# Self-attention on TensorE in steps of two units: score pair, eight transposes, two chunks of head outputs

## The chip, the cores and the metric

The kernel runs on one core of a Trainium2 chip. Times are device microseconds (us) of that core for one execution. Engines are named as the profile names them: PE is TensorE's matmul side (PEld its weight loads), ACT is ScalarE, DVE is VectorE, POOL is GpSimd, SP is SyncE. L485 is line 485 of the kernel before.

## What is computed

The kernel is a decoder of six stages over `x` of shape (4, 512, 128): self-attention, cross-attention, a mixture of experts, a gated decay attention, a second cross-attention and a second mixture of experts, each followed by a residual sum and a layer norm. The change lies in the first stage only:

```python
x = (latents - mu) * jax.lax.rsqrt(var + 1e-05) * ln_gamma + ln_beta
q = (x @ Wq).reshape(b, s, HEADS, DIM_HEAD).transpose(0, 2, 1, 3)    # 16 heads of 64
k = (x @ Wk).reshape(b, s, HEADS, DIM_HEAD).transpose(0, 2, 1, 3)
v = (x @ Wv).reshape(b, s, HEADS, DIM_HEAD).transpose(0, 2, 1, 3)
scores = jnp.einsum('bhqd,bhkd->bhqk', q * scale, k * scale)
weights = jax.nn.softmax(scores.astype(jnp.float32), axis=-1)
out = jnp.einsum('bhqk,bhkd->bhqd', weights, v)
return out.transpose(0, 2, 1, 3).reshape(b, s, HEADS * DIM_HEAD) @ Wo
```

All of it is in fp32.

## The kernel before

The program is written per engine; the order in each engine's block is the order of issue, and semaphores tie the engines together. Nothing reorders instructions between blocks.

**Units and groups.** Self-attention is cut into 256 units: four batches of 64. Unit u is one head and one tile of 128 queries against all 512 keys. Units 2n and 2n+1 are the two heads of a pair on the same query tile. Eight units, a group g = u // 8, are one pair of heads on its four query tiles; there are 32 groups. Below, a place in a group is called j = u % 8, and S(u), X(u), T(u), pt(u) stand for the unit's steps.

**The way of a unit.** S(u): PE makes the scores of both heads of a pair in one go (`a_scores`, L477, called for even u), 4 matmul records of 64 contraction rows. DVE takes the row maximum (`a_max`, L1317). X(u): ACT makes the exponential with its row sum (`a_exp`, L940). DVE inverts the row sum (`a_norm`, L1324), POOL multiplies by it (L1813). T(u): PE transposes the unit's four 128 x 128 squares into one bank (`a_turn`, L489). pt(u): ACT copies that bank to SBUF (`a_pt`, L947). O: PE multiplies with the values (`a_out`, L496), once per group and chunk k of 128 keys, four chunks of 4 matmul records of 64 columns each, into bank 5. ACT copies bank 5 out (`a_o`, L956).

**Banks.** Scores use banks 0 to 2 in rotation, by unit; so S(u) must wait for X(u - 2). Transposes use banks 3 and 4, by u % 2; so T(u) must wait for pt(u - 2) (`take` in L491 puts the wait on `a_pt` in front of it). The projections Q and K (`a_qk`, L471, line L475 in the trace), V (`a_v`, L463, L468), the transposes of the layer norm and the output projection of the batch before (`tail`, L432) share banks 6 and 7 in strict turns (`take_next`, L347): each waits for the copy by ACT of the one issued two before it.

**Order on PE before** (loop at L517): at step u the extra work of that step (a piece of `tail`, Q at j = 2, K at j = 4, V at the steps of `V_STEPS`, L280), then S(u) if u is even, then T(u - 4), then, from step 13 on, chunk (u - 13) % 8 of the head outputs if that is under 4. So chunks 0 to 3 of a group stand at j = 5, 6, 7 and 0.

**Order on ACT** (L976): at step u `tail`, V's copy, X(u), then the copy of Q at j = 2 (`a_q`, `a_evac` L932), of K at j = 5 (`a_k`, the same line), of bank 5 at j = 1, then pt(u - 4). The copy of K for group g + 2 also waits until the last score pair of group g is done, because it overwrites that group's keys.

**Order on DVE** (L1340): at step u first `a_norm(u - 1)`, which waits for X(u - 1), then `a_max(u)`, then `tail` and the layer norm's work.

Of the kernel before, what the change touches and what calls it, by code (L numbers as in the profile page):

```python
# [33 lines left out]
NB = 4  # L34
S = 512
NT = S // P
# [10 lines left out]
UNITS = H * NT  # L47
# [31 lines left out]
def decoder(nc, T):  # L79

    with ExitStack() as ctx:
# [5 lines left out]
        def sem(name):  # L87
            if name not in sems:
                sems[name] = ctx.enter_context(nc.semaphore(name))
            return sems[name]  # L90
# [128 lines left out]
        def v3(ap, n):  # L219
            return ap.rearrange("p (n k) -> p n k", n=n)  # L220


        wqA, wkA, wvA, woA = (W0[:, i * 1024:(i + 1) * 1024] for i in range(4))
# [13 lines left out]
        def out_w(ph):  # L237
            return {0: woA, 1: woB, 3: woD, 4: woE}[ph]

        def o_slot(w, p):  # L240

            if w // NB == 3:
                s = (8 * (w % NB) + p) % 12
                return OT[:, s, :] if s < 8 else oxD[s - 8]
            return OT[:, p, :]
# [27 lines left out]
        def tail_steps(w):  # L273
            if w // NB in (1, 4) and w % NB < NB - 1:
                return (0, 2, 4, 6, 8)

            return TAIL[(w + 1) // NB]


        V_STEPS = ((49, 51, 57, 59), (17, 19, 25, 27))  # L280

        def yn(w):

            return w if w < PC else w - NB

        def out_pieces(w):

            return 4 if w < NB - 1 else 1
# [9 lines left out]
        def loaded(eng, what, n=1):  # L298
            eng.wait_ge(dma_in[what], 16 * n)
# [37 lines left out]
        def take(pe, i, reader, value):  # L337

            if i in owner:
                s, n = owner[i]  # L340
                pe.wait_ge(s, n)
            owner[i] = (reader, value)
            return bank[i]
# [3 lines left out]
        def take_next(pe, key, reader, value):  # L347

            i = 6 + turn[0] % 2
            turn[0] += 1  # L350
            where[key] = bank[i]
            return take(pe, i, reader, value)
# [64 lines left out]
        def _(pe):  # L417
            mm = nc.tensor.matmul

            def tail(w, s, last=False):  # L420

                ph = w // NB
                at = tail_steps(w)
                k, pieces = s - at[0], out_pieces(w)
                if 0 <= k < pieces and ph in (0, 1, 3, 4):
                    n = 4 if ph == 4 else 8
                    if k == 0:

                        pe.wait_ge(sem({0: "a_o", 1: "B_o", 3: "d_og", 4: "E_o"}[ph]), n * (w % NB + 1))
                        take_next(pe, ("y", w), yT_ready, yn(w) + 1)  # L430
                    for p in range(k * n // pieces, (k + 1) * n // pieces):
                        m = mm(where["y", w][:, :], out_w(ph)[:, p * P:(p + 1) * P], o_slot(w, p),  # L432
                               start=(p == 0), stop=(p == n - 1))
                    if k == pieces - 1:
                        m.then_inc(y_ready, 1)
                if s == at[1]:
                    pe.wait_ge(yT_ready, yn(w) + 1)
                    out = take_next(pe, ("yt", w), sem("sum_done"), yn(w) + 1)
                    for t in range(NT):
                        m = nc.tensor.transpose(out[:, t * P:(t + 1) * P], yT[:, t * P:(t + 1) * P], ident)  # L440
                    m.then_inc(yt_ready, 1)
                if s == at[4]:
                    turn_x(w)

            def turn_x(w):

                pe.wait_ge(x_ready, w + 1)
                out = take_next(pe, ("xT", w), xT_ready, w + 1)
                b = w % NB
                for t in range(NT):  # L450
                    m = nc.tensor.transpose(out[:, t * P:(t + 1) * P], x_all[:, 4 * b + t, :], ident)
                m.then_inc(xTp_ready, 1)


            def a_norm_T(b):

                pe.wait_ge(sem("a_xn"), b + 1)
                out = take_next(pe, ("a_xn", b), sem("a_xnT"), b + 1)
                for t in range(NT):
                    m = nc.tensor.transpose(out[:, t * P:(t + 1) * P], v3(xn, NT)[:, t, :], ident)  # L460
                m.then_inc(sem("a_xnp"), 1)

            def a_v(b, hf, t):  # L463

                n = 8 * b + 4 * hf + t
                pe.wait_ge(sem("a_xnT"), b + 1)
                out = take_next(pe, ("a_v", n), sem("a_vs"), n + 1)
                mm(out[:, :], xnT[b % 2][:, t * P:(t + 1) * P], wvA[:, hf * S:(hf + 1) * S], start=True, stop=True)\  # L468
                    .then_inc(sem("a_vp"), 1)

            def a_qk(g, w, ready, done):  # L471
                b, p = g // 8, g % 8
                pe.wait_ge(sem("a_xnT"), b + 1)
                out = take_next(pe, (ready, g), sem(done), g + 1)
                mm(out[:, :], w[:, p * P:(p + 1) * P], xnT[b % 2], start=True, stop=True).then_inc(sem(ready), 1)  # L475

            def a_scores(u):  # L477
                g, t = u // 8, (u // 2) % 4
                if u % 8 == 0:

                    pe.wait_ge(sem("a_qe"), g + 1)
                    pe.wait_ge(sem("a_ke"), g + 1)
                out = [take(pe, (u + hh) % 3, sem("a_e"), u + hh + 1) for hh in range(2)]
                for hh in range(2):
                    m = mm(out[hh][:, :], qA[g % 2][HALF[hh], t * P:(t + 1) * P], kA[g % 2][HALF[hh], :],  # L485
                           start=True, stop=True)
                m.then_inc(sem("a_s"), 1)

            def a_turn(u):  # L489
                pe.wait_ge(sem("a_n"), u + 1)  # L490
                out = take(pe, 3 + u % 2, sem("a_pt"), u + 1)  # L491
                for k in range(NT):
                    m = nc.tensor.transpose(out[:, k * P:(k + 1) * P], pA[u % 5][:, k * P:(k + 1) * P], ident)  # L493
                m.then_inc(sem("a_t"), 1)

            def a_out(g, k):  # L496
                b, p = g // 8, g % 8
                if k == 0:
                    pe.wait_ge(sem("a_pt"), 8 * g + 8)
                    pe.wait_ge(sem("a_vs"), 8 * b + 4 * (p // 4) + 4)  # L500
                    take(pe, 5, sem("a_o"), g + 1)
                for hh in range(2):
                    m = mm(bank[5][hh * DH:(hh + 1) * DH, :], v3(vA[p // 4], NT)[:, k, (2 * (p % 4) + hh) * DH:(2 * (p % 4) + hh + 1) * DH],  # L503
                           v3(ptA[(2 * g + hh) % 4], NT)[:, k, :], start=(k == 0), stop=(k == NT - 1))
                if k == NT - 1:
                    m.then_inc(sem("a_pv"), 1)
# [7 lines left out]
            for t in range(NT):  # L514
                a_v(0, 0, t)
            NU = NB * UNITS
            for u in range(NU + 9):  # L517
                b, s, g, j = u // UNITS, u % UNITS, u // 8, u % 8
                if u < NU:
                    if u == UNITS:  # L520
                        loaded(pe, "woA")
                    if b:
                        tail(b - 1, s)
                    if s == 30 and b + 1 < NB:
                        a_norm_T(b + 1)
                    if j == 2 and g + 1 < 32:
                        a_qk(g + 1, wqA, "a_qp", "a_qe")
                    if j == 4 and g + 2 < 32:
                        a_qk(g + 2, wkA, "a_kp", "a_ke")
                    if s in V_STEPS[0] and b + 1 < NB:  # L530
                        a_v(b + 1, 0, V_STEPS[0].index(s))
                    if s in V_STEPS[1]:
                        a_v(b, 1, V_STEPS[1].index(s))
                    if u % 2 == 0:
                        a_scores(u)
                if 4 <= u < NU + 4:
                    a_turn(u - 4)
                if u >= 13:

                    h, k = divmod(u - 13, 8)  # L540
                    if k < NT and h < 32:
                        a_out(h, k)


# [1439 lines left out]
```

## Time and profile before

| what | us |
|---|---|
| median of 3 runs (1633.65 to 1636.2) | 1636.05 |
| the profiled execution, its own time | 1640.13 |
| its span, from the first to the last instruction | 1638.3 |
| self-attention, from the first score pair to the last head outputs | about 21 to 550 |

Of the span PE is busy for 1328.1 us (81%), DVE for 854.0, ACT for 831.8 and POOL for 546.9. A line of the timeline reads: start, time from that start to the end of the last instruction merged into the line, engine, line, operation, output <- input, forms, count, and in brackets the idle time of the engine before it with what ended it. The ends of matmuls are modelled and overlap the next matmul; the distance between two starts is what the first one holds the engine for.

### The profile page before, as it was taken

The page shows a single profiled execution, that of the slowest core. Times are in us where ns is not written, and L with a number is a line of the kernel's source. Part 1 is how long each engine was busy: PE and PEld are TensorE (multiplying, and loading weights), DVE is VectorE, ACT ScalarE, POOL GpSimd, SP SyncE. Part 2 cuts the span into 40 slices and gives each one's busy share as a digit, 9 for nine tenths or more (in the row PEclk, how much of TensorE's full clock was granted, in tenths as well). Part 3 has the DMA queues.
Part 4 walks back from the last instruction along what each step waited for, and adds up shares of the span by engine and source line. Part 5 has one row for each costly group of instructions (what it writes and reads, how often), then busy time and mean ns, then how long its engine had stood idle before and what let it go on. Part 6 is the DMA issues. An engine that isn't in the chain of part 4 may idle for free.

```text
span 1638.3 us, 22200 instructions
## 1 busy us (share of the span) xinstructions
PE 1328.1 (81%) x6934; PEld 743.1 (45%) x6934; DVE 854.0 (52%) x2721; ACT 831.8 (51%) x1885; POOL 546.9 (33%) x511
## 2 busy tenths in 40 slices
PE   5999999999999888876549658788889897796460
PEld 2434434444443345444248636455555554444250
DVE  3444543453344354674522176777666775557525
ACT  4777677677677535453225345446454552343130
POOL 3455455455445411323454342100000110112253
PEclk9999999999999989987769879889999997887685
DMA  9000000000000000000259600000000000000172
GB/s 371 23 1 1 1 1 1 1 1 1 1 1 1 1 0 1 1 1 13 85 187 339 222 26 9 6 1 1 1 1 1 1 1 0 1 1 7 37 234 59
DMA packets 35074, 67.30 MB, mean 41 GB/s; under 512 B 5424, under 2 KB 21296, under 8 KB 33808
## 3 DMA queue, kind: packets, MB, share of 16 engines
q1 hardware_dynamic: 29328, 54.37, 9.6%
q0 software_dynamic: 5056, 10.36, 2.1%
q8 instruction: 58, 0.95, 0.2%
q10 hardware_dynamic: 576, 1.16, 0.2%
q14 instruction: 56, 0.46, 0.1%
HBM read 47.71 MB, written 18.15 MB: 40 GB/s over the span
## 4 chain that ended last, share of the span: by engine, by line
PE 60%; DVE 19%; issue 8%; ACT 5%; DMA 5%; POOL 2%; DVEq 0%; ACTq 0%; POOLq 0%
PE bank L503 8%; PE bank L485 7%; PE bank L493 6%; PE bank L432 5%; DMA work<-xs,xi 4%; PE bank L608 3%; PE bank L806 3%; PE bank L475 3%; PE bank L565 3%; PE bank L579 3%; PE bank L802 2%; DVE work L1321 2%; PE bank L594 1%; PE bank L672 1%; POOL xs L1866 1%
## 5 line engine op out<-in xcount | busy, mean ns | idle before, releaser
L1813 POOL TENSOR_TENSOR work<-work 128x512 f32<-128x512 f32 x256 | 266.5, 1041 | 277.6 <-DVE work L1329 277.6
L944 ACT ACTIVATE work<-bank,work 128x512 f32<-128x512 f32 x256 | 176.5, 689 | 117.8 <-DVE work L1321 117.6
L1321 DVE TENSOR_REDUCE work<-bank 128x1 f32<-128x512 f32 x256 | 176.7, 690 | 76.7 <-PE bank L485 75.8
L493 PEld LDWEIGHTS bank<-cst,work 128*128 128x128 f32 x1024 | 110.5, 140 | 164.4 <-issue 106.0
L493 PE MATMUL bank<-cst,work 128*128 128x128 f32 x1024 | 160.0, 283 | 6.6 <-ACT work L952 6.1
L1329 DVE RECIPROCAL work<-work 128x1 f32<-128x1 f32 x256 | 41.9, 164 | 222.6 <-ACT work L944 222.3
L952 ACT ACTIVATE work<-bank 128x512 f32<-128x512 f32 x256 | 152.6, 596 | 0.5 <-PE bank L493 0.5
L1914 POOL TENSOR_TENSOR work<-work 128x512 f32<-128x512 f32 x32 | 40.9, 1277 | 332.4 <-PE bank L806 312.6
L485 PE MATMUL bank<-work 64*128 64x512 f32 x512 | 144.5, 641 | 3.4 <-ACT work L944 3.4
L1853 POOL TENSOR_TENSOR work<-work 128x1232 f32<-128x1232 f32 (+1 forms) x32 | 55.5, 1735 | 250.3 <-DVE work L1401 250.2
L503 PE MATMUL bank<-work 128*64 128x512 f32 x512 | 137.4, 617 | 0.7 <-ACT work L952 0.7
L1383 DVE TENSOR_REDUCE work<-bank 128x6 f32<-128x462 f32 (+1 forms) x80 | 38.9, 536 | 111.7 <-PE bank L579 111.6
L1108 ACT ACTIVATE work<-bank,W 128x128 f32<-128x128 f32 x202 | 58.6, 368 | 75.3 <-PE bank L672 63.3
L432 PE MATMUL bank<-OT,W 128*128 128x512 f32 x208 | 94.0, 595 | 0.7 <-DVE am L1506 0.7
L594 PE MATMUL bank<-cst,work 128*128 128x128 f32 x384 | 60.8, 311 | 28.2 <-POOL work L1853 20.8
L485 PEld LDWEIGHTS bank<-work 64*128 64x128 f32 x512 | 38.7, 184 | 97.0 <-issue 60.5
L1055 ACT ACTIVATE work<-bank 128x512 f32<-128x512 f32 x96 | 53.1, 595 | 54.7 <-PE bank L594 54.2
L1148 ACT ACTIVATE work<-bank,work 128x128 f32<-128x128 f32 x256 | 72.4, 384 | 14.5 <-PE bank L754 10.1
L763 PE MATMUL bank<-W_low 128*128 128x512 f32 x96 | 46.8, 487 | 40.6 <-DVE work L1643 19.2
L1893 POOL DMA_INDIRECT work<-xs,xi x62 | 58.7, 947 | 61.6 <-PE bank L663 45.3
L475 PE MATMUL bank<-W 128*128 128x512 f32 x128 | 68.1, 617 | 6.2 <-ACT work L932 3.9
L579 PE MATMUL bank<-work 128*128 128x154 f32 x384 | 60.5, 309 | 13.8 <-DVE work L1388 13.8
(232 smaller groups left out, 2550.0 us busy)
## 6 DMA issues: line engine op xcount, KB each, us to landing
W<-in_wC SPq DMA_DIRECT2D x39, 578.0 KB
xs<-gat SPq DMA_DIRECT2D x9, 1024.0 KB, 16.5
W<-in_wF SPq DMA_DIRECT2D x23, 321.0 KB
ys<-work SPq DMA_DIRECT2D x62, 64.0 KB
x_all<-in_x SPq DMA_DIRECT2D x4, 256.0 KB, 8.7
W<-in_L_attn_Wq SPq DMA_DIRECT2D x2, 512.0 KB, 5.5
W<-in_L_attn_Wv SPq DMA_DIRECT2D x2, 512.0 KB, 7.6
W<-in_L_attn_Wo SPq DMA_DIRECT2D x2, 512.0 KB, 9.0
```

The costliest lines, as they stand in the source:

```text
L432: m = mm(where["y", w][:, :], out_w(ph)[:, p * P:(p + 1) * P], o_slot(w, p), start=(p == 0), stop=(p == n - 1))
L475: mm(out[:, :], w[:, p * P:(p + 1) * P], xnT[b % 2], start=True, stop=True).then_inc(sem(ready), 1)
L485: m = mm(out[hh][:, :], qA[g % 2][HALF[hh], t * P:(t + 1) * P], kA[g % 2][HALF[hh], :], start=True, stop=True)
L493: m = nc.tensor.transpose(out[:, k * P:(k + 1) * P], pA[u % 5][:, k * P:(k + 1) * P], ident)
L503: m = mm(bank[5][hh * DH:(hh + 1) * DH, :], v3(vA[p // 4], NT)[:, k, (2 * (p % 4) + hh) * DH:(2 * (p % 4) + hh + 1) * DH], v3(ptA[(2 * g + ...
L579: m = mm(out[:, (p % 3) * 2 * C:(p % 3 + 1) * 2 * C], v3(qTB, NPAIR)[:, p, t * P:(t + 1) * P], kd, start=True, stop=True)
L594: m = nc.tensor.transpose(out[:, i * P:(i + 1) * P], pB[u % 3][:, h * C:h * C + P], ident)
L944: A(pA[u % 5], bank[u % 3][:, :], ACT.Exp, bias=nmax[:, u % 8:u % 8 + 1], accum_out=rsum[0][:, u % 8:u % 8 + 1]).then_inc(sem("a_e"), 1)
L952: A(v3(ptA[h % 4], NT)[:, :, t * P:(t + 1) * P], v3(bank[3 + u % 2][:, :], NT), ACT.Copy)\
L1148: i = A(dmD[g % 2][:, (NT * hh + c) * P:(NT * hh + c + 1) * P], bank[1 - hh][:, c * P:(c + 1) * P], ACT.Exp, scale=-1.0, bias=lcD[b % 2][: ...
L1321: V.tensor_reduce(nmax[:, u % 8:u % 8 + 1], bank[u % 3][:, :], AX, ALU.max, negate=True)\
L1813: G.tensor_tensor(pA[u % 5], pA[u % 5], rsum[1][:, u % 8:u % 8 + 1].to_broadcast([P, S]), ALU.mult)\
```

## The change

Only PE's loop changes. It now runs over even u. A step does the extra work of step u and of step u + 1 (the same calls, in the same order among themselves, V ahead of Q and K within one), then S(u), then T(u - 4) and T(u - 3) with nothing between them, then, at j = 6, chunks 0 and 1 of the head outputs, and at j = 0, chunks 2 and 3. ACT, DVE, POOL and SP keep their instructions and their order, and no bank, buffer or wait is another.

```diff
-            for u in range(NU + 9):
-                b, s, g, j = u // UNITS, u % UNITS, u // 8, u % 8
+            for u in range(0, NU + 10, 2):
+                b, g = u // UNITS, u // 8
                 if u < NU:
                     if u == UNITS:
                         loaded(pe, "woA")
-                    if b:
-                        tail(b - 1, s)
-                    if s == 30 and b + 1 < NB:
-                        a_norm_T(b + 1)
-                    if j == 2 and g + 1 < 32:
-                        a_qk(g + 1, wqA, "a_qp", "a_qe")
-                    if j == 4 and g + 2 < 32:
-                        a_qk(g + 2, wkA, "a_kp", "a_ke")
-                    if s in V_STEPS[0] and b + 1 < NB:
-                        a_v(b + 1, 0, V_STEPS[0].index(s))
-                    if s in V_STEPS[1]:
-                        a_v(b, 1, V_STEPS[1].index(s))
-                    if u % 2 == 0:
-                        a_scores(u)
-                if 4 <= u < NU + 4:
-                    a_turn(u - 4)
-                if u >= 13:
-
-                    h, k = divmod(u - 13, 8)
-                    if k < NT and h < 32:
+                    for s in (u % UNITS, u % UNITS + 1):
+                        if b:
+                            tail(b - 1, s)
+                        if s == 30 and b + 1 < NB:
+                            a_norm_T(b + 1)
+                        if s in V_STEPS[0] and b + 1 < NB:
+                            a_v(b + 1, 0, V_STEPS[0].index(s))
+                        if s in V_STEPS[1]:
+                            a_v(b, 1, V_STEPS[1].index(s))
+                        if s % 8 == 2 and g + 1 < 32:
+                            a_qk(g + 1, wqA, "a_qp", "a_qe")
+                        if s % 8 == 4 and g + 2 < 32:
+                            a_qk(g + 2, wkA, "a_kp", "a_ke")
+                    a_scores(u)
+                for v in (u - 4, u - 3):
+                    if 0 <= v < NU:
+                        a_turn(v)
+                h, i = divmod(u - 14, 8)
+                if 0 <= h < 32 and i in (0, 2):
+
+                    for k in (i, i + 1):
                         a_out(h, k)
```

What stands on PE in a row, in a group without V (here units 34 to 39 of the first batch). L485 is a score pair, L493 x4 one unit's transposes, L475 Q or K, L503 x2 one chunk of the head outputs. Before:

```order
L485 MATMUL bank<-work 128x512 x2
L493 MATMUL bank<-cst,work 128x128 x8
L475 MATMUL bank<-W 128x512
L485 MATMUL bank<-work 128x512 x2
L493 MATMUL bank<-cst,work 128x128 x8
L503 MATMUL bank<-work 64x512 x2
L485 MATMUL bank<-work 128x512 x2
L493 MATMUL bank<-cst,work 128x128 x4
L503 MATMUL bank<-work 64x512 x2
L493 MATMUL bank<-cst,work 128x128 x4
L503 MATMUL bank<-work 64x512 x2
```

The same place on PE in the changed kernel:

```order
L485 MATMUL bank<-work 128x512 x2
L493 MATMUL bank<-cst,work 128x128 x8
L475 MATMUL bank<-W 128x512
L485 MATMUL bank<-work 128x512 x2
L493 MATMUL bank<-cst,work 128x128 x8
L485 MATMUL bank<-work 128x512 x2
L493 MATMUL bank<-cst,work 128x128 x8
L503 MATMUL bank<-work 64x512 x4
```

Between the third-last and the second-last score pair (j = 4 and j = 6) a chunk has gone; behind the pair at j = 6 the chunk that stood between the two units' transposes has moved behind both.

The second place is PE's beginning of a group with V (units 16 to 20; L468 is V). Before:

```order
L485 MATMUL bank<-work 128x512 x2
L493 MATMUL bank<-cst,work 128x128 x4
L503 MATMUL bank<-work 64x512 x2
L468 MATMUL bank<-W 128x512
L493 MATMUL bank<-cst,work 128x128 x4
L475 MATMUL bank<-W 128x512
L485 MATMUL bank<-work 128x512 x2
L493 MATMUL bank<-cst,work 128x128 x4
L468 MATMUL bank<-W 128x512
L493 MATMUL bank<-cst,work 128x128 x4
L475 MATMUL bank<-W 128x512
L485 MATMUL bank<-work 128x512 x2
```

And in the changed kernel:

```order
L468 MATMUL bank<-W 128x512
L485 MATMUL bank<-work 128x512 x2
L493 MATMUL bank<-cst,work 128x128 x8
L503 MATMUL bank<-work 64x512 x4
L475 MATMUL bank<-W 128x512
L468 MATMUL bank<-W 128x512
L485 MATMUL bank<-work 128x512 x2
L493 MATMUL bank<-cst,work 128x128 x8
L475 MATMUL bank<-W 128x512
L485 MATMUL bank<-work 128x512 x2
```

Each V has moved from behind a score pair to the front of it: the first to the front of S at j = 0, the second to the front of S at j = 2, straight behind Q.

## Rows read from the trace of the kernel before

**Rows 1.** Busy time by stretch: us, each engine's busy us, granted clock, DMA.
```profile
21.00:550.00 529.00, 513.86 (x2298) 210.95 (x2298) 233.08 (x659) 385.37 (x899) 266.71 (x257) 1.00 0.05 19
600.00:640.00 40.00, 33.91 (x166) 20.78 (x167) 18.01 (x31) 22.65 (x33) 8.99 (x4) 0.91 0.00 1
```

**Rows 2.** Timeline of PE, a group without V: start, us, operation, [idle <- releaser].
```profile
280.70 1.13 PE L485 MATMUL bank<-work 64*128 64x512 f32 x4
...
284.80 1.13 PE L485 MATMUL bank<-work 64*128 64x512 f32 x4
285.86 1.09 PE L493 MATMUL bank<-cst,work 128*128 128x128 f32 x8
286.79 1.02 PE L475 MATMUL bank<-W 128*128 128x512 f32 x2
287.75 1.13 PE L485 MATMUL bank<-work 64*128 64x512 f32 x4
...
289.76 0.63 PE L493 MATMUL bank<-cst,work 128*128 128x128 f32 x4 [0.29 <-ACT work L952]
290.31 1.08 PE L503 MATMUL bank<-work 128*64 128x512 f32 x4
291.32 1.13 PE L485 MATMUL bank<-work 64*128 64x512 f32 x4
...
295.57 0.70 PE L485 MATMUL bank<-work 64*128 64x512 f32 x2
```

**Rows 3.** Timeline of ACT in the same group.
```profile
286.70 0.69 ACT L944 ACTIVATE work<-bank,work 128x512 f32<-128x512 f32 x1 [0.74 <-DVE work L1321]
...
287.38 0.59 ACT L932 ACTIVATE work<-bank 128x512 f32<-128x512 f32 x1
...
288.34 0.70 ACT L944 ACTIVATE work<-bank,work 128x512 f32<-128x512 f32 x1
...
289.00 0.61 ACT L952 ACTIVATE work<-bank 128x512 f32<-128x512 f32 x1
289.96 0.69 ACT L944 ACTIVATE work<-bank,work 128x512 f32<-128x512 f32 x1 [0.35 <-DVE work L1321]
...
292.56 0.60 ACT L932 ACTIVATE work<-bank 128x512 f32<-128x512 f32 x1 [0.20 <-PE bank L485]
```

**Rows 4.** Timeline of PE and ACT in a group with V.
```profile
112.42 1.13 PE L485 MATMUL bank<-work 64*128 64x512 f32 x4
...
118.98 1.02 PE L468 MATMUL bank<-W 128*128 128x512 f32 x2
119.84 0.60 PE L493 MATMUL bank<-cst,work 128*128 128x128 f32 x4
...
120.01 0.59 ACT L932 ACTIVATE work<-bank 128x512 f32<-128x512 f32 x1
...
120.74 1.10 PE L475 MATMUL bank<-W 128*128 128x512 f32 x2 [0.30 <-ACT work L932]
...
122.83 1.09 PE L493 MATMUL bank<-cst,work 128*128 128x128 f32 x8
123.85 1.08 PE L503 MATMUL bank<-work 128*64 128x512 f32 x4
...
129.11 0.70 PE L485 MATMUL bank<-work 64*128 64x512 f32 x2
```

**Rows 5.** Timeline at the start, where no head outputs lie between transposes and scores.
```profile
26.67 0.69 ACT L944 ACTIVATE work<-bank,work 128x512 f32<-128x512 f32 x1 [0.82 <-DVE work L1321]
...
27.59 1.13 PE L485 MATMUL bank<-work 64*128 64x512 f32 x4 [1.10 <-ACT work L944]
...
30.79 1.13 PE L485 MATMUL bank<-work 64*128 64x512 f32 x4 [1.04 <-ACT work L944]
```

**Rows 6.** Timeline of PE in cross-attention: head outputs in one run.
```profile
681.76 3.96 PE L608 MATMUL bank<-work 128*64 128x512 f32 x16
685.65 2.36 PE L579 MATMUL bank<-work 128*128 128x154 f32 x16
```

## The prediction

> **What bounds the kernel now.** I read the busy times by stretch first, then the timeline of one group of eight units on PE and on ACT, then the places where PE is known to wait. In self-attention PE is busy for 513.86 of 529 us at a granted clock of 1.00, full speed [rows 1]. So PE's own order sets the time there, and what it waits for is small: in a group without V one wait, for the copy pt of ACT in front of the second unit's transposes, [0.29 <-ACT work L952] [rows 2]. A group without V lasts 295.57 - 280.70 = 14.87 us from score pair to score pair [rows 2], one with V 129.11 - 112.42 = 16.69 us [rows 4]. The rest of the program is not touched.
>
> Behind PE stands a second cycle that is nearly as long. X of one unit, the inverse and the next maximum on DVE, then X of the next: 286.70 to 288.34 to 289.96, that is 1.64 and 1.62 us per unit [rows 3], or 13.0 us per group against PE's 14.87. A change that lets PE wait on this cycle at one point and leaves it nothing to do meanwhile loses quickly.
>
> **Prices, from starts to starts.** Score pair to transposes 1.06 (284.80 to 285.86), two units' transposes 0.93 (285.86 to 286.79), Q or K ahead of scores 0.96 [rows 2]. Two units' transposes ahead of head outputs 1.02 (122.83 to 123.85), a projection ahead of an operation of the full array 0.86 (118.98 to 119.84) [rows 4]. One chunk of head outputs 1.01 (290.31 to 291.32), transposes that had to wait 0.55 (289.76 to 290.31) [rows 2]. Two chunks in one run are not in this stage; cross-attention runs four of the same shape in 685.65 - 681.76 = 3.89, which makes 1.95 for two [rows 6]; the ends are 1.89 (a little less switching) and 2.02 (nothing saved). I take 1.95.
>
> The waits: X(u) starts 1.90 after the start of S(u) (284.80 to 286.70) [rows 2, 3]. A score pair can follow X(u - 2) by 0.92 (26.67 to 27.59) [rows 5]. X holds ACT for 0.68 (286.70 to 287.38), a copy for 0.48 (287.38 to 288.34 holds two) [rows 3]. Transposes can follow the start of the copy that frees their bank by 0.76 (289.00 to 289.76) [rows 2, 3]. K can follow the start of Q's copy by 0.73 (120.01 to 120.74) [rows 4].
>
> **What the change saves.** In a group without V the order is now S TT OO, Q S TT, K S TT, S TT OO. Without any wait that is (1.06 + 1.02 + 1.95 + 0.96) + (1.06 + 0.93 + 0.96) + (1.06 + 0.93) + (1.06 + 1.02 + 1.95) = 4.99 + 2.95 + 1.99 + 4.03 = 13.96, which is 0.91 less than 14.87: about half of it the wait, the rest fewer changes between score, output and full-array matmuls.
>
> **What it costs, group without V.** I follow one group with S at j = 0 at time 0.
> - S(2) at 4.99 (X(0) at 1.90 frees it long before). X(2) at 6.89, X(3) 1.64 later at 8.53, X(4) 1.62 later at 10.15.
> - S(4) at 7.94, its transposes; PE has nothing left at 9.93. Before, a chunk of head outputs lay here. S(6) needs X(4): 10.15 + 0.92 = 11.07, a wait of 1.14. The start of the trace shows this very pattern, two score pairs with only transposes between, 3.20 apart (27.59 to 30.79) with [1.04 <-ACT work L944] [rows 5].
> - X(5) at 11.77; ACT then copies K (12.45) and pt(1) (12.93). K's copy waited 0.20 for the score pair before [rows 3]; now S(6), at 11.07, is early enough, since the copy could follow it by 292.56 - 291.32 = 1.24 [rows 2, 3], at 12.31.
> - T(2) at 12.13, T(3) would come at 12.62, but its bank is free only at 12.93 + 0.76 = 13.69: a wait of 1.07. Before, chunk 1 stood between the two and covered it. The chunks now queue behind T(3), although they are ready.
> - Output chunks at 13.69 + 0.55 = 14.24, next group at 14.24 + 1.95 = 16.19.
>
> So 16.19 against 14.87: **+1.32 per group**. The waits (2.21) are more than the saving (0.91). Nothing later in the group makes it up, because X(6) and X(7) run ahead of the next S. Who waits for the late T(3)? Its pt and the next S(0), and with it everything.
>
> **Group with V.** The first V stands ahead of S(0), the second between Q and S(2). OO ends at 4.03, Q 0.86, V 0.96: S(2) at 5.85 instead of 5.01. V's bank is free by then (its copy on ACT starts about 3.06). X(2) at 7.75, Q's copy at 8.43, K at 8.43 + 0.73 = 9.16, while PE has been ready since 5.85 + 1.06 + 0.93 = 7.84: a wait of 1.32, where the kernel before had 119.84 + 0.44 to 120.74, some 0.46, because V stood behind the pair. S(4) at 10.12, X(4) 12.02, S(6) 12.94, X(5) 13.64, K's copy 14.32, pt(1) 14.80, T(3) 15.56, outputs 16.11 to 18.06, the next V 0.96: 19.02. Against 16.69: **+2.33 per group**.
>
> **The sum.** V is at 14 groups (two per batch for the second half, two more in three batches for the first). Three groups carry pieces of the output projection, which stand ahead of the score pairs and cover the first wait; I give them 0.3 each. Groups 0, 1 and 31 fill and drain the pipeline; the first two run at the X cycle already, the last has the T wait: 1 us in all. The other 12 are plain. 12 x 1.32 + 14 x 2.33 + 1 + 1 = 15.8 + 32.6 + 2 = 50.4 us. The profiled execution would go from 1640.1 to 1690.5. The median of the runs lies 4.1 lower, so 1636.05 + 50.4 = **1686**. The ends of the unknown price of OO are -0.06 and +0.07 on 26 groups, 2 us; that V groups with layer norm work on DVE lose less takes off up to 10.
>
> **Rivals.**
> 1. *The switches are what costs, and PE stays ahead (faster).* Were the waits on ACT absent, each of 26 groups would give 0.91 back: 24 us, 1612. It decides where the two waits per group stay under 0.91. For it: PE is 97% busy [rows 1]. Against it: the wait of 0.29 that is there already with more cover, and the 1.04 at the start [rows 2, 5]. The Trainium skill, TensorEngine Tiling (Array Packing), section Key Properties, says that changing the tiling mode drains TensorE, which speaks for this rival; the rows agree with a small size: transposes for two units take 0.93 ahead of a full-array operation [rows 2] and 1.02 ahead of outputs [rows 4].
> 2. *Only the score wait counts.* If T(3) does not wait (ACT frees its bank in time, because X(5) comes sooner than I have it), each of 26 groups keeps 1.07 of the loss: 28 us less, 1658.
> 3. *PE's clock falls.* With gaps of over 1 us twice a group the granted clock could drop as it does at 600 to 640, 33.91 of 40 busy and 0.91 [rows 1]. At 0.91 some 18% of the stretch runs at half speed (1.2 of 2.4 GHz), up to 529 x 0.18 / 2 = 48 us more: 1734. Against it: gaps of 1.04 to 1.10 at the start stand within the stretch that keeps 1.00 [rows 1, 5]. The Trainium skill, TensorE: Matmul & The Clock Gate, tells of kernels whose clock swings because PE idles briefly between groups while banks cycle; by that the time would be this rival's, and the trace so far does not show it for gaps of this size.
>
> **Chances.** The forecast 0.86, the first rival 0.05, the second 0.05, the third 0.04. A measurement of this kernel can tell 0.2% (3.3 us) from no change. Slower by more: 0.93 (forecast, second and third, less a little for a mix of the first two); within 0.2%: 0.02; faster: 0.05. The range, 1656 to 1702, takes the forecast with its ends and reaches the second rival.
>
> **What the profile after would show.** In a group without V: S at j = 4 and j = 6 about 3.1 apart with an idle PE released by ACT L944 (its line then one lower); T at j = 6 in two runs 1.6 apart, the second released by the copy pt; groups of 16.2 and 19.0; K released by Q's copy after some 1.3; a clock of 1.00; everything behind self-attention as before but 50 us later. I am wrong if the second transposes start 0.5 behind the first at j = 6, if groups are under 14.9, or if the clock in self-attention is below 1.00.

## The result

| kernel | median us | runs | ratio to before, 95% interval |
|---|---|---|---|
| before | 1636.12 | 1633.65 to 1641.84 | |
| changed | 1690.6 | 1690.08 to 1692.51 | 1.033 (1.0302 to 1.0358) |

The change costs 54.5 us of the median; 50.4 were forecast (1686, range 1656 to 1702). All of it is in self-attention. From the first score pair to the last head output the stage took 531.3 us before and takes 585.1 now, 53.9 more. The first score pair starts 1.0 later, and the rest of the program behind the stage, the same code, took 1085.5 us before and 1080.5 after, so the span grew by 50.0 only; in the eleven kernels of this study that rest lies between 1077 and 1086. That the 50.0 of the span come so near to the 50.4 forecast is therefore chance; the stage's 53.9 is the number to set beside it. Below, kernels are compared by the stage and by the group of eight units, and their medians beside it.

Busy times by stretch of the changed kernel, to set beside [rows 1]: PE does as many instructions (x2298) in 583 us as before in 529, its busy time has even fallen a little, and the clock has stayed at 1.00.

```profile
21.00:604.00 583.00, 510.32 (x2298) 217.65 (x2296) 231.58 (x659) 381.58 (x899) 266.08 (x256) 1.00 0.04 17
```

Who PE waited for in the stage, in the changed kernel (engine, tile and line, releaser: us in total, times, longest):

```profile
PE bank L493 <- ACT work L953: 31.6, 47, 0.9
PE bank L485 <- ACT work L945: 20.3, 33, 1.1
PE bank L475 <- ACT work L933: 16.2, 14, 1.2
PE bank L468 <- ACT xT_all L908: 3.8, 3, 1.7
```

Before, the three first lines held 6.1, 3.4 and 3.9 us. Each is one wait that the prediction named: transposes for their bank (pt), score pairs for an exponential, K for Q's copy. The fourth it did not name.

A group without V on PE, timeline of the changed kernel (columns as in [rows 2]; ACT's lines are one higher than before):

```profile
308.55 1.13 PE L485 MATMUL bank<-work 64*128 64x512 f32 x4
...
316.50 1.13 PE L485 MATMUL bank<-work 64*128 64x512 f32 x4
317.56 0.66 PE L493 MATMUL bank<-cst,work 128*128 128x128 f32 x4
318.51 0.63 PE L493 MATMUL bank<-cst,work 128*128 128x128 f32 x4 [0.29 <-ACT work L953]
319.64 1.13 PE L485 MATMUL bank<-work 64*128 64x512 f32 x4 [0.50 <-ACT work L945]
320.70 0.66 PE L493 MATMUL bank<-cst,work 128*128 128x128 f32 x4
322.23 0.63 PE L493 MATMUL bank<-cst,work 128*128 128x128 f32 x4 [0.87 <-ACT work L953]
322.79 1.94 PE L503 MATMUL bank<-work 128*64 128x512 f32 x8
324.65 1.13 PE L485 MATMUL bank<-work 64*128 64x512 f32 x4
```

From pair to pair 324.65 - 308.55 = 16.10 us, against 14.87 [rows 2]. The pairs at j = 4 and j = 6 stand 3.14 apart (316.50, 319.64), with only transposes between; the transposes at j = 6 come in two runs 1.53 apart (320.70, 322.23), and the chunks queue behind the second. Before, the pair at j = 6 came 3.57 behind the one at j = 4, but a chunk was done in between [rows 2]. The bracket shows less than the whole wait, because the modelled end of the matmul before it reaches into it; starts are what to go by.

Why the second transposes are late stands on ACT:

```profile
318.71 0.69 ACT L945 ACTIVATE work<-bank,work 128x512 f32<-128x512 f32 x1 [0.35 <-DVE work L1322]
...
320.33 0.69 ACT L945 ACTIVATE work<-bank,work 128x512 f32<-128x512 f32 x1 [0.35 <-DVE work L1322]
...
321.01 0.59 ACT L933 ACTIVATE work<-bank 128x512 f32<-128x512 f32 x1
321.48 0.60 ACT L953 ACTIVATE work<-bank 128x512 f32<-128x512 f32 x1
```

X(4) at 318.71 releases the pair at 319.64, 0.93 later; X(5), K's copy, then pt(1) at 321.48, and the transposes 0.75 behind it.

The third wait, in a group with V, from the timeline of PE; the last line is ACT's copy of Q there:

```profile
127.52 1.13 PE L485 MATMUL bank<-work 64*128 64x512 f32 x4
128.58 1.09 PE L493 MATMUL bank<-cst,work 128*128 128x128 f32 x8
130.83 1.10 PE L475 MATMUL bank<-W 128*128 128x512 f32 x2 [1.16 <-ACT work L933]
131.85 1.13 PE L485 MATMUL bank<-work 64*128 64x512 f32 x4
...
130.10 0.59 ACT L933 ACTIVATE work<-bank 128x512 f32<-128x512 f32 x1
```

K (L475) starts 0.73 behind the start of Q's copy. Eight transposes hold PE for 0.93, so it was ready at 129.51 and stood for 1.32.

### The profile page after: what moved, and what is told of

Read it like the earlier page. It is cut to its first block, busy times and chain, and to the rows that moved or that the text cites. A ratio compares the mean times of both kernels' runs of the same rounds, so it can differ in the third digit from the quotient of the medians.

```text
span 1688.3 us, 22200 instructions
## 1 busy us (share of the span) xinstructions
PE 1320.0 (78%) x6934; PEld 748.9 (44%) x6934; DVE 853.2 (51%) x2721; ACT 827.8 (49%) x1885; POOL 545.9 (32%) x511
## 4 chain that ended last, share of the span: by engine, by line
PE 53%; DVE 21%; issue 10%; ACT 8%; DMA 6%; POOL 2%; DVEq 0%; ACTq 0%; POOLq 0%
PE bank L503 7%; PE bank L432 5%; PE bank L485 5%; DMA work<-xs,xi 5%; DVE work L1322 4%; PE bank L493 3%; PE bank L807 3%; PE bank L475 3%; PE bank L609 3%; PE bank L566 3%; ACT work L945 3%; PE bank L580 3%; PE bank L803 2%; PE bank L468 2%; ACT work L933 2%
## 5 line engine op out<-in xcount | busy, mean ns | idle before, releaser
L493 PE MATMUL bank<-cst,work 128*128 128x128 f32 x1024 | 150.0, 281 | 32.3 <-ACT work L953 31.6
L493 PEld LDWEIGHTS bank<-cst,work 128*128 128x128 f32 x1024 | 108.7, 140 | 140.5 <-issue 103.5
L485 PE MATMUL bank<-work 64*128 64x512 f32 x512 | 144.5, 639 | 20.3 <-ACT work L945 20.3
L503 PE MATMUL bank<-work 128*64 128x512 f32 x512 | 123.8, 605 | 0.7 <-ACT work L953 0.7
L475 PE MATMUL bank<-W 128*128 128x512 f32 x128 | 71.8, 647 | 18.5 <-ACT work L933 16.2
L485 PEld LDWEIGHTS bank<-work 64*128 64x128 f32 x512 | 39.5, 184 | 100.8 <-issue 52.7
L595 PE MATMUL bank<-cst,work 128*128 128x128 f32 x384 | 59.3, 305 | 26.6 <-POOL work L1854 19.1
L1149 ACT ACTIVATE work<-bank,work 128x128 f32<-128x128 f32 x256 | 72.3, 384 | 14.9 <-PE bank L755 10.5
## 6 DMA issues: line engine op xcount, KB each, us to landing
xs<-gat SPq DMA_DIRECT2D x9, 1024.0 KB, 16.2
```

The source lines that it names most:

```text
L595: m = nc.tensor.transpose(out[:, i * P:(i + 1) * P], pB[u % 3][:, h * C:h * C + P], ident)
L1149: i = A(dmD[g % 2][:, (NT * hh + c) * P:(NT * hh + c + 1) * P], bank[1 - hh][:, c * P:(c + 1) * P], ACT.Exp, scale=-1.0, bias=lcD[b % 2][: ...
```

## The experiments

The length of a group is from the start of its first score pair to that of the next group's; "with V" is such a stretch that holds two V's; the stage is from the first score pair to the last head output, against 531.3 before, in one profiled execution of each kernel. Each kernel's runs share a chip with runs of the kernel before.

| kernel | median (before beside it) | stage vs before | plain group | with V |
|---|---|---|---|---|
| before | | 0 | 14.88 | 16.69 |
| changed | 1690.6 (1636.1) | +53.9 | 16.10 | 19.10 |
| e1 alternating | 1674.6 (1634.3) | +39.8 | 15.64 | 18.64 |
| e2 extra work behind | 1670.3 (1634.3) | +36.8 | 16.10 | 18.04 |
| e3 copies paired | 1659.8 (1634.3) | +28.4 | 15.53 | 18.04 |
| e4 chunks at j = 4 | 1682.5 (1634.3) | +51.8 | 16.10 | 18.04 |
| e9 both cures | 1654.7 (1636.3) | +18.3 | 14.84 (two of 15.19) | 17.10 |
| e8 only extra work in front | 1659.2 (1633.9) | +23.3 | 14.88 | 17.70 |
| e5 rebalanced | **1607.7** (1633.9) | **-27.8** | 13.79 | 15.51 |
| e6 rebalanced, chunks at j = 6 | 1636.6 (1633.9) | +2.1 | 15.04 | 16.45 |
| e7 rebalanced, alternating | 1624.6 (1633.9) | -11.5 | 14.39 | 16.11 |

**e1: transposes and chunks alternate.**

```diff
-                for v in (u - 4, u - 3):
-                    if 0 <= v < NU:
-                        a_turn(v)
-                h, i = divmod(u - 14, 8)
-                if 0 <= h < 32 and i in (0, 2):
-                    for k in (i, i + 1):
-                        a_out(h, k)
+                h, i = divmod(u - 14, 8)
+                for v, k in ((u - 4, i), (u - 3, i + 1)):
+                    if 0 <= v < NU:
+                        a_turn(v)
+                    if 0 <= h < 32 and i in (0, 2):
+                        a_out(h, k)
```

> The changed kernel with one thing undone: within a step the transposes and the chunks alternate again, T(u-4), chunk, T(u-3), chunk, at j = 6 and j = 0. Steps of two units, their extra work in front, and the places of the chunks by step stay. My theory (the two waits on ACT): the wait of T at j = 6 for its bank (1.07 per group) is covered by the chunk, S at j = 6 still waits for X at j = 4; a plain group falls from 16.10 to about 15.56, one with V by 0.63, in all 26 x 0.6 = 15 us less than the changed kernel: 1675. Rival A (the longer runs are worth something in themselves and the loss lies in the work moved in front of the pairs): nothing gained, and 0.15 per change of mode lost on 64 places, 1690 to 1700. Rival B (the run of eight transposes is the whole loss): back to 1640.

Measured 1674.6, ratio 1.0234 (1.0212 to 1.0255), 16 us under the changed kernel, 14 by the stage. A chunk now stands between the two units' transposes at j = 6; the step S(6) to S(0) fell from 5.01 to 4.25, and PE's waits for pt in the stage from 31.6 to 6.0 us, what they were before. The wait of the pair at j = 6 stayed: 3.14, 20.2 us in all. So the wait for the bank is real, it is worth 0.76 per group less the 0.30 that alternating costs at j = 0, and it is not the whole loss.

**e2: the odd unit's extra work behind the pair.** The extra work of step u stays in front of S(u), that of u + 1 goes behind the chunks.

```diff
-                    for s in (u % UNITS, u % UNITS + 1):
-                        ...
+                    extra(u, u % UNITS)
                     a_scores(u)
...
                         a_out(h, k)
+                if u < NU:
+                    extra(u, u % UNITS + 1)
```

> The changed kernel with one thing undone: the extra work of the odd unit of a step (V, pieces of the output projection, copies' transposes) stands behind the step's score pair, transposes and chunks, not in front of the pair. Transposes and chunks stay in runs. My theory: plain groups stay at 16.1; a group with V loses one projection's 0.96 of delay, since the first V is now covered by the wait of the copies and K waits less for Q's copy; 14 x 0.96 = 13 us less: 1677. Rival A (the work moved in front of the pairs is the whole loss): about 1640. Rival B (only the runs matter): unchanged, 1690.

Measured 1670.3, ratio 1.0212 (1.0194 to 1.023), 20 us under the changed kernel, 17 by the stage, where 13 were expected. The groups behaved as worked out: plain 16.10, with V 19.10 to 18.04, and PE's wait of K for Q's copy fell from 16.2 to 3.0 us in the 14 groups. What I had left out is that the groups of units 24 to 31 in the second and third batch, where the new x of the batch before is transposed, and those with the output projection gain too, 20.35 to 19.06 and 23.27 to 22.38.

**e3: the two copies paired on ACT.** PE is as in the changed kernel.

```diff
-                if u >= 4:
-                    a_pt(u - 4)
+                if u >= 4 and u % 2 == 0:
+                    a_pt(u - 4)
+                    a_pt(u - 3)
```

> PE as in the changed kernel. On ACT the two copies of a pair of transposed units, pt(u-4) and pt(u-3), now both stand behind X(u), in the time in which ACT waits for the second maximum, instead of one behind X(u) and one behind X(u+1). My theory (T waits for its bank, that is for pt): T at j = 6 no longer waits (1.07 less), though X(3) comes 0.5 later behind Q's copy, so that S at j = 6 waits 0.5 longer; a plain group 16.1 to 15.6, one with V 19.1 to 18.0; 7 + 15 = 22 us less than the changed kernel: 1668. Rival C (the weight loads in front of the transposes, put down to POOL by the trace, wait for POOL's product and not for the bank): nothing changes, 1690.

Measured 1659.8, ratio 1.0149 (1.0126 to 1.0171), 31 us under the changed kernel by the medians, 25.5 by the stage, where 22 were expected. PE's timeline in a plain group:

```profile
304.65 1.13 PE L485 MATMUL bank<-work 64*128 64x512 f32 x4
305.71 1.09 PE L493 MATMUL bank<-cst,work 128*128 128x128 f32 x8
308.28 1.13 PE L485 MATMUL bank<-work 64*128 64x512 f32 x4 [1.48 <-ACT work L945]
309.34 1.09 PE L493 MATMUL bank<-cst,work 128*128 128x128 f32 x8
```

Transposes run eight in a row at j = 4 and j = 6, and no transposes wait for a copy any more in the stage's list. The wait for the pair at j = 6 grew from 3.14 to 3.63 between starts, as Q's copy and two pt's now lie ahead of X(3). The rival is out: POOL's work is as before, and the waits of the transposes are gone. The trace still puts 47.0 us of the weight loads' idle time in front of the transposes down to POOL (37.1 in the changed kernel), though the matmuls behind them now start without a wait; so that line does not show what holds the transposes up.

**e4: chunks 0 and 1 at j = 4.**

```diff
-                h, i = divmod(u - 14, 8)
-                if 0 <= h < 32 and i in (0, 2):
-                    for k in (i, i + 1):
+                h, i = divmod(u - 12, 8)
+                if 0 <= h < 32 and i in (0, 4):
+                    for k in (i // 2, i // 2 + 1):
```

> The changed kernel with chunks 0 and 1 in the step j = 4 instead of j = 6; they stay in one run, as all else. My theory: S at j = 6 no longer waits for X at j = 4, as 1.9 us of work stand in between (1.14 less); T at j = 6 still waits for its bank, longer than before, because the copy of K now waits for the later score pair; a plain group about 15.5, one with V 18.0; 7 + 13 = 20 us less: 1670. Rival B (the run of eight transposes is the whole loss): nothing changes, 1690. If both of my waits can be had at once, this and the paired copies add up.

Measured 1682.5, ratio 1.0281 (1.0262 to 1.03): 8 us gained where 20 were expected; in the stage 2. Two short falls of the clock are in it (last section). The wait for the score pair went as expected (20.3 to 6.8 us in the stage), but a plain group stayed at 16.10. Timeline of PE:

```profile
252.85 1.13 PE L485 MATMUL bank<-work 64*128 64x512 f32 x4
253.91 0.66 PE L493 MATMUL bank<-cst,work 128*128 128x128 f32 x4
254.95 0.63 PE L493 MATMUL bank<-cst,work 128*128 128x128 f32 x4 [0.39 <-ACT work L952]
...
265.81 1.13 PE L485 MATMUL bank<-work 64*128 64x512 f32 x4
266.87 0.66 PE L493 MATMUL bank<-cst,work 128*128 128x128 f32 x4
268.28 0.63 PE L493 MATMUL bank<-cst,work 128*128 128x128 f32 x4 [0.75 <-ACT work L952]
```

and of ACT at the same place:

```profile
267.05 0.60 ACT L932 ACTIVATE work<-bank 128x512 f32<-128x512 f32 x1 [1.06 <-PE bank L485]
267.54 0.59 ACT L952 ACTIVATE work<-bank 128x512 f32<-128x512 f32 x1
```

The pair at j = 6 is now at 265.81, later behind the one at j = 4 than before, and K's copy on ACT waits 1.06 for it (it must not overwrite keys in use). pt(1) and everything else on ACT stand behind that copy. This I had counted at j = 6; that ACT carries the delay on into the next group, where the second transposes at j = 0 wait as well (253.91 to 254.95), I had not, and it is the missing 0.6 of the group. Of the cures tried on the changed kernel this one shows best that a wait removed on PE can come back through an in-order engine beside it.

**e9: e3 and e4 together.**

> The changed kernel with both cures at once, and nothing else: chunks 0 and 1 in the step j = 4, and the two copies of transposes both behind X(u) on ACT. Q, K, V and the extra work of odd units stay where the change has them. My theory: the chunks at j = 4 alone brought little because T then waited longer for its bank (behind K's copy, which waits for the later score pair); with the copies paired that wait is gone and the two cures add up to more than their sum. From the measured prices: plain group, X(2) at 6.81, X(4) at 10.55, S(6) at 11.81 without a wait, X(6) at 13.81, next group at 14.73; group with V 16.9. That is 12 x -0.1 + 14 x 0.25 against the kernel before, and 6 us for the work moved in front at the layer norm's and output projection's places: about 1642. Rival (the cures overlap: one wait is what counts, and it is gone with the paired copies): as the paired copies alone, 1660.

Measured 1654.7, ratio 1.012 (1.0093 to 1.0146). The groups are as worked out, 14.84 (14.73 expected) and 17.10 or 16.98 (16.9): a plain group gains 1.26, more than twice the 0.57 that e3 alone and the nothing that e4 alone bring it. So in the plain groups the cures do more together than apart, and the rival, in which one wait is all, is wrong there. The 1642 was missed by 13 us, most of it where the layer norm's and the output projection's work stands in front of a pair: the two groups of units 24 to 31 in the second and third batch take 22.0 and 22.8 us against 17.9 before, those with the output projection 23.4 against 22.0. I had given these places 6 us. Two short falls of the clock, told of at the end, are in it.

**e8: only the extra work in front.** The kernel before, with transposes and chunks unit by unit as they were, but the extra work of u and u + 1 in front of S(u). The edit is shown against the changed kernel.

```diff
-                for v in (u - 4, u - 3):
-                    if 0 <= v < NU:
-                        a_turn(v)
-                h, i = divmod(u - 14, 8)
-                if 0 <= h < 32 and i in (0, 2):
-
-                    for k in (i, i + 1):
-                        a_out(h, k)
+                for v in (u, u + 1):
+                    if 4 <= v < NU + 4:
+                        a_turn(v - 4)
+                    if v >= 13:
+                        h, k = divmod(v - 13, 8)
+                        if k < NT and h < 32:
+                            a_out(h, k)
```

> The kernel before with one part of the change alone: the extra work of unit u + 1 stands with that of u in front of the score pair; transposes and chunks stay where they were, unit by unit. My theory: plain groups stay at 14.9; a group with V loses about one projection less what the K wait had cost before, 0.9: 14 x 0.9 = 13 us, and 4 us at the places of the layer norm's and output projection's transposes: 1651. Rival (it costs only beside the longer runs): 1634.

Measured 1659.2, ratio 1.0158 (1.0128 to 1.0188): +25 us where +17 were expected, +23 in the stage. Plain groups did not change (14.88), those with V went from 16.69 to 17.70, and the groups ahead of one, which now hold its first V, from 14.87 to 15.94, with K's wait for Q's copy at 15.2 us in the stage, against 3.9. The rest is at the odd places. Timeline of PE and ACT at unit 26 of the second batch:

```profile
210.04 0.60 PE L451 MATMUL bank<-cst,x_all 128*128 128x128 f32 x4
210.70 1.10 PE L475 MATMUL bank<-W 128*128 128x512 f32 x2
214.04 1.10 PE L468 MATMUL bank<-W 128*128 128x512 f32 x2 [2.24 <-ACT xT_all L907]
215.06 1.65 PE L485 MATMUL bank<-work 64*128 64x512 f32 x4
```

```profile
211.65 0.69 ACT L944 ACTIVATE work<-bank,work 128x512 f32<-128x512 f32 x1 [1.10 <-DVE work L1321]
...
213.29 0.61 ACT L907 ACTIVATE xT_all<-bank 128x512 f32<-128x512 f32 x1
```

V of unit 27 (L468) needs the bank that the transposes of the new x at unit 26 (L451, `turn_x`) hold until ACT copies them (L907). ACT does that at its own step 26, behind the exponential of unit 25, while PE already stands in front of the score pair of unit 26. With V behind the pair, as before, the wait fell into time that PE had work for. It is K's wait for Q's copy once more, with another pair of users of banks 6 and 7.

**e5: rebalanced.** If the two waits and the bank turns are the loss, the runs of the change should pay once all are covered. On PE chunks 0 and 1 at j = 4, Q in front of j = 0, K in front of j = 4, odd units' work behind the pair; on ACT the copies paired and the others behind the second exponential of a pair:

```diff
-        V_STEPS = ((49, 51, 57, 59), (17, 19, 25, 27))
+        V_STEPS = ((51, 55, 59, 63), (19, 23, 27, 31))
...
-                        if s % 8 == 2 and g + 1 < 32:
+                if s % 8 == 0 and g + 1 < 32:
...
+                    a_exp(u)
+                    if j == 1 and g >= 2:
+                        a_o(g - 2)
+                    if j == 1 and g + 1 < 32:
+                        a_q(g + 1)
+                    if j == 5 and g + 2 < 32:
+                        a_k(g + 2)
...
+                if u >= 4 and u % 2 == 0:
+                    a_pt(u - 4)
+                    a_pt(u - 3)
```

> Runs of eight transposes and of two chunks, as in the change, but with both waits covered: the two copies of transposes both behind X(u) on ACT; chunks 0 and 1 at j = 4, chunks 2 and 3 at j = 0; Q in front of the pair at j = 0 and K in front of that at j = 4, so that each step without chunks is followed by a projection; the extra work of odd units behind the pair; V at odd units 3 and 7 of its groups; ACT copies Q and bank 5 behind X at j = 1, K behind X at j = 5. My theory: with the waits covered PE is the bound again and the fewer changes between kinds of matmul show: a plain group 13.9 (4.0 + 2.95 + 4.0 + 2.95) against 14.87 before, one with V 15.6 to 15.8 against 16.69: 12 x 0.95 + 14 x 1.0 = 25 us less than before, 1609. Rival (the cycle of exponential and maximum, 1.63 per unit and 13.0 per group, leaves no slack and binds at other places): within 8 us of before.

Measured 1607.7, ratio 0.9839 (0.9815 to 0.9863): 26 us faster than before, 83 faster than the changed kernel, with the change's runs in it. Timeline of PE over a plain group:

```profile
268.56 1.13 PE L485 MATMUL bank<-work 64*128 64x512 f32 x4
269.62 1.09 PE L493 MATMUL bank<-cst,work 128*128 128x128 f32 x8
270.64 1.94 PE L503 MATMUL bank<-work 128*64 128x512 f32 x8
272.51 1.13 PE L485 MATMUL bank<-work 64*128 64x512 f32 x4
...
282.35 0.70 PE L485 MATMUL bank<-work 64*128 64x512 f32 x2
```

None of PE's lines in this group, those left out included, has a bracket: every start follows from the instruction before it, and 282.35 - 268.56 = 13.79 us per group.

**e6: the same with chunks 0 and 1 back at j = 6.**

> As the rebalanced kernel, but chunks 0 and 1 back at j = 6, where the change has them. My theory: T no longer waits for its bank, but S at j = 6 again waits for X at j = 4, as only transposes lie between: from S at j = 2 to S at j = 6 6.08 (1.90 + 1.64 + 1.62 + 0.92), a plain group about 14.9 against 13.9, 1.0 more on 26 groups: 26 us more than the rebalanced kernel, about 1635. Rival (only the transposes' bank mattered): as the rebalanced kernel.

Measured 1636.6, ratio 1.0012 (0.9997 to 1.0028), 29 us more than e5; a plain group 15.04 against 14.9 expected. PE's waits for exponentials in front of score pairs are 33.8 us in the stage, against 7.9 in e5, and there is none for transposes. So the cover of the score pair at j = 6, taken alone, is worth 1.25 us a plain group.

**e7: the same as e5, alternating.**

> As the rebalanced kernel, but transposes and chunks alternate again within a step (T, chunk, T, chunk). This measures what the longer runs are worth where nothing waits. My theory: 0.14 for the first chunk's way out and 0.15 for the second transposes' way in, 0.30 per run (5.31 against 5.01 for the step at j = 0 in the runs with and without), two runs per group, 0.6 per group: 32 x 0.6 = 19 us more than the rebalanced kernel, about 1628. Rival (the runs are worth nothing in themselves, the gain of the rebalanced kernel is the wait that the kernel before had): same as the rebalanced kernel.

Measured 1624.6, ratio 0.9943 (0.9926 to 0.9961), 17 us more than e5; 16.2 in the stage. Where nothing waits, two units' transposes and two chunks take 3.19 us alternating and 2.89 in runs (283.94 to 287.13 in e7, 269.62 to 272.51 in e5), 0.30 a time and 0.60 a group. So of the 26 us by which e5 is faster than the kernel before, the longer runs gave some 17; the other 9 (11.5 in the stage) come with e7 too, from the places of the other work:

```profile
283.94 0.66 PE L493 MATMUL bank<-cst,work 128*128 128x128 f32 x4
284.52 1.08 PE L503 MATMUL bank<-work 128*64 128x512 f32 x4
285.53 0.66 PE L493 MATMUL bank<-cst,work 128*128 128x128 f32 x4
286.12 1.08 PE L503 MATMUL bank<-work 128*64 128x512 f32 x4
287.13 1.13 PE L485 MATMUL bank<-work 64*128 64x512 f32 x4
```

## Why the prediction was right, point by point

- **The saving.** 0.91 per plain group was the forecast, half of it fewer changes between kinds of matmul. The e5 group, which has none of the waits, is 1.09 shorter than before, 0.60 of it shown by e7 to be the runs. Two chunks in one run took 1.86 (322.79 to 324.65), not 1.95; the lower end of the range, 1.89, was nearer.
- **The score pair at j = 6** waits for X(4): 3.14 between the pairs, 3.13 forecast (7.94 to 11.07). Shown by e6 against e5.
- **The second transposes at j = 6** wait for their bank: 1.53 between the two runs, 1.56 forecast. Shown by e1 and e3, the second of which left PE alone.
- **K waits for Q's copy** in a group with V: 1.32 (129.51 to 130.83), 1.32 forecast. Shown by e2, which puts V behind the pair again and leaves 3.0 of 16.2 us, and by e8, which brings 15.2 us of it into the kernel before.
- **A plain group** 16.10 against 16.19, **one with V** 19.10 against 19.02. (The working has 5.01 once where its own sum gives 4.99; nothing hangs on it.) The 12 plain groups grew by 14.2 in all, where 15.8 were forecast.
- **The groups with V** hold the first term that was mis-sized. 2.33 each counts both V's, but a group's first V now stands in front of its S(0), and so in the stretch of the group ahead: 17.16 for group 5, 16.10 for a plain one, 1.06 for the V. Booked to V in all seven such places, the eight groups without layer norm or output work of the batch before cost 18.4 together, against 18.6. The six with it (groups 2 and 3 of the second to fourth batch) cost 18.0, against 14.0, where I had even allowed for less. Most of that stands where V of unit 27 needs the bank that the transposes of the new x at unit 26 hold: 3.8 us of waiting in three places, which stood in no step. Group 11 grew by 2.49, group 7, which has no such wait, by 1.35.
- **The groups with the output projection** grew by 1.23 each (22.04 to 23.27), but 1.06 of it is such a first V. That leaves 0.2 each, where I gave 0.3: the pieces do cover the score wait (3.80 between the pairs at j = 4 and j = 6). With the odd units' work behind the pair, e2, they take 22.38, 0.34 over the kernel before.
- **The ends of the stage** are the second term that was mis-sized: 1 was forecast, and the last group took 2.1 more and group 1, without its V, 0.7. The terms measure 14.2 + 18.4 + 18.0 + 0.5 + 2.8 = 53.9, the forecast ones 15.8 + 18.6 + 14.0 + 1 + 1 = 50.4: 5.8 too little in two of them, 2.3 too much in the others, so part of the closeness is luck.
- **The rivals.** The switches are real, at 0.30 a run, and smaller than the waits; the first rival's mechanism shows itself only in e5. The second, in which the transposes do not wait, is wrong by the 1.53 above. The clock did not fall in the changed kernel: it was granted at 1.00 (2.4 GHz) over the whole stage, with waits of up to 1.7 us in the list above.

What stays open: the shares of the loss are not additive. By the stage, undoing the extra work's place gives 17 us, alternating 14, pairing the copies 26, covering the pair 2, or 10 beside the paired copies, and adding the extra work's place to the kernel before costs 23. The sum of such parts depends on what else waits, as e4 and e9 show, so no split of the 54 us into three causes is claimed. The short falls of the clock (last section) are in these stage times; by an estimate from the 1.6 us of one of them in e6, they hold some 3 us in e4, e6 and e9 and half of that in e3 and e8.

## What to carry to other kernels

A longer run on the bound engine saves its switches (here 0.30 us per run) but takes away the work that stood between two dependent steps. Before merging, list for each run what the engine waits for at its front, with the start that releases it, and check that each interval still holds as much work as the slowest chain through the other engines (here 1.90 + 0.92 from score pair to score pair, 1.63 per unit through exponential and maximum). If it doesn't, move the other work with the runs: the same runs cost 54 us with the work left where it was. With the chunks, projections and copies spread the kernel was 26 us faster than before, and 17 of these are what the runs give there (e7 against e5).

## What was not expected of the hardware

The clock is not quite safe in this stage. The changed kernel kept 1.00 to the end of it, and so did e1, e2, e5 and e7, but e4, e6 and e9 have a short stretch of half speed (1.2 GHz) in the midst of it twice each, e3 and e8 once, each at or just behind one of their longest waits (1.72 to 2.38 in the bracket). In e6 that is the second half of a group where DVE's layer norm work delays the exponentials. Its busy times over ten such microseconds (granted clock 0.83), and its timeline of PE there:

```profile
190.00:200.00 10.00, 7.92 (x31) 3.77 (x31) 7.06 (x27) 7.57 (x19) 4.98 (x6) 0.83 0.01 2
```

```profile
192.72 1.09 PE L493 MATMUL bank<-cst,work 128*128 128x128 f32 x8
195.89 1.42 PE L485 MATMUL bank<-work 64*128 64x512 f32 x4 [2.08 <-ACT work L950]
197.24 1.97 PE L493 MATMUL bank<-cst,work 128*128 128x128 f32 x8
199.14 2.35 PE L503 MATMUL bank<-work 128*64 128x512 f32 x8
201.42 1.13 PE L468 MATMUL bank<-W 128*128 128x512 f32 x2
```

Behind a run of eight transposes and a wait of 2.08 the pair takes 1.35 instead of 1.06, eight transposes 1.90 instead of 1.02 and two chunks 2.28 instead of 1.87: 1.6 us lost at one place. That is part of why the groups of e6 at this place take 19.4 us, where that of the fourth batch, with a clock of 1.00, takes 17.9. In e4 the same follows on a wait of 2.38 for the copy of the new x, in front of which Q and four transposes ran. So what the third rival feared exists here, behind waits longer than the 1.14 that the forecast looked at, and it cost some 3 us in a kernel, not 48. A wait of that length does not always bring it. The same place in the fourth batch of e6 has the same wait of 2.08 behind eight transposes (at 467.76), and there the clock was granted at 1.00: the pair took 1.06, eight transposes 1.03 and two chunks 1.86. In e8 the waits of 2.24 at 214.04 and at 356.89 stand at the same place of two batches, and only the first has a fall behind it. The changed kernel has two waits of 1.68 and no fall. A fall was not made or undone on purpose; that the waits bring it is read from where it stands, and what decides between two equal waits stays open. The Trainium skill, TensorE: Matmul & The Clock Gate, section "A second HAM failure mode: psum-queue depth-cycling", tells of a kernel whose clock swings because PE idles briefly between groups of matmuls. In this stage the traces agree only as far as single falls behind single long waits; the changed kernel, with 94 shorter waits of up to 1.2 us, kept 1.00.

The rest of the program, which no experiment touched, took between 1076.8 and 1086.0 us in the profiled executions, with a mean granted clock of 0.87 to 0.88. The runs of one kernel spread as far (1604.5 to 1613.4 for e5), more than the 3.3 us that are 0.2%. A stage measured from its own first to its own last instruction told 0.1 us per group apart, in one execution of each kernel.
